# Layer norm's scaling and the turned maxima's copy on ScalarE, two pieces of VectorE's behind the next maxima, in a two-layer block

## Time and profile before

| | us |
|---|---|
| median of 3 runs (1610.04 to 1612.97) | 1611.84 |
| the profiled execution's own time | 1606.22 |
| its span, first to last instruction | 1604.5 |
| TensorE, VectorE, ScalarE, GpSimd busy | 1459.2, 1338.2, 1129.7, 578.4 |
| mean granted TensorE clock | 0.956 |

### The profile page before, as it was taken

One profiled execution on the slowest core, in us unless ns is written; L12 is line 12 of the kernel. 1 busy time (PEld: TensorE's weight loads), 2 busy tenths in 40 slices (PEclk: granted clock), 3 DMA queues, 4 the chain that ended last, 5 costly groups with the idle time before them and its releaser, 6 DMA issues.

```text
span 1604.5 us, 34217 instructions
## 1 busy us (share of the span) xinstructions
PE 1459.2 (91%) x10557; PEld 583.9 (36%) x10557; DVE 1338.2 (83%) x3450; ACT 1129.7 (70%) x2580; POOL 578.4 (36%) x531
## 2 busy tenths in 40 slices
PE   3978989999999899989999999989999988989986
PEld 1112344443333544432333444333433432323332
DVE  6999877789887698999888789889878779978991
ACT  2267678788787467777878767768878845765675
POOL 3002302103253456440242263660152464554443
PEclk8599999999999899999999999999999977989998
DMA  6403273333271452221451135123372100600000
GB/s 172 102 8 100 73 184 110 106 87 91 88 183 52 120 116 83 59 82 36 134 120 51 37 113 134 49 82 99 111 165 82 39 26 2 152 9 15 2 2 14
DMA packets 169833, 131.84 MB, mean 82 GB/s; under 512 B 31597, under 2 KB 143158, under 8 KB 169654
## 3 DMA queue, kind: packets, MB, share of 16 engines
q1 hardware_dynamic: 165562, 121.26, 28.5%
q0 software_dynamic: 4096, 8.40, 1.7%
HBM read 88.50 MB, written 40.50 MB: 80 GB/s over the span
## 4 chain that ended last, share of the span: by engine, by line
PE 58%; DVE 26%; issue 6%; ACT 5%; POOL 3%; DMA 1%; SPq 0%; another core or an unknown queue 0%; DVEq 0%; ACTq 0%; POOLq 0%
PE ring L542 38%; PE pO L542 17%; DVE mparts L1201 15%; PE ring L545 3%; ACT PR L854 3%; DVE junk L1205 2%; DVE xr L1381 1%; DVE stats L1251 1%; ACT hid L925 1%; DVE hs L1493 1%; DVE xr L1501 1%; DVE am L1414 1%; DMA b1r<-in_b 1%; ACT parts L548 0%; DVE hs L1489 0%
## 5 line engine op out<-in xcount | busy, mean ns | idle before, releaser
L854 ACT ACTIVATE PR<-ring 128x512 f32<-128x512 f32 (+3 forms) x1792 | 882.4, 557 | 344.8 <-PE ring L542 333.7
L1201 DVE TENSOR_REDUCE mparts<-ring 128x1 f32<-128x512 f32 x1280 | 808.5, 682 | 84.4 <-PE ring L542 77.1
L542 PE MATMUL ring<-QX,KX 50*128 50x512 bf16 (+3 forms) x1792 | 543.7, 366 | 77.2 <-DVE mparts L1201 35.5
L542 PE MATMUL ring<-KX,QX 48*128 48x512 bf16 (+3 forms) x1792 | 556.8, 374 | 14.2 <-DMA QX<-scratch 14.1
L542 PE MATMUL pO<-PR,VX 128*18 128x512 f32 (+3 forms) x3584 | 444.0, 568 | 6.5 <-ACT PR L854 5.2
L542 PEld LDWEIGHTS ring<-QX,KX 50*128 50x128 bf16 x1792 | 127.5, 94 | 609.0 <-ACT PR L854 220.3
L1205 DVE CUSTOM_DVE_ANT_0 junk<-ring,diag 128x384 bf16<-128x384 f32 (+3 forms) x512 | 228.8, 486 | 46.0 <-PE ring L542 41.2
L811 POOL TENSOR_SCALAR bq<-bq 128x352 f32<-128x352 f32 (+1 forms) x40 | 47.2, 1179 | 349.7 <-ACT bq L964 349.3
L784 POOL DMA_INDIRECT rows_in<-xn,at x64 | 63.7, 996 | 228.8 <-PE pO L542 144.8
L542 PEld LDWEIGHTS ring<-KX,QX 48*128 48x128 bf16 x1792 | 127.3, 94 | 33.6 <-DVE mparts L1201 17.9
L925 ACT ACTIVATE hid<-ring,b1r 128x128 f32<-128x128 f32 x368 | 105.0, 369 | 27.7 <-PE ring L542 26.2
(11 more groups left out here) (165 smaller groups left out, 1349.8 us busy)
## 6 DMA issues: line engine op xcount, KB each, us to landing
w1r<-in_w SPq DMA_DIRECT2D x92, 256.0 KB
w2r<-in_w SPq DMA_DIRECT2D x92, 256.0 KB
scratch<-parts SPq DMA_DIRECT2D x48, 256.0 KB, 3.3
scratch<-parts SPq DMA_DIRECT2D x96, 128.0 KB, 2.3
KX<-scratch SPq DMA_DIRECT2D x64, 192.0 KB, 4.4
QX<-scratch SPq DMA_DIRECT2D x128, 96.0 KB, 5.0
xg<-rows_in SPq DMA_DIRECT2D x92, 64.0 KB
rows_out<-yx SPq DMA_DIRECT2D x92, 64.0 KB
```

The source lines that it names most:

```text
L542: return nc.tensor.matmul(dst, lhsT, rhs, start=start, stop=stop, **kw)
L854: nc.scalar.activation(PR[:, n % 2, HALF * j + off:HALF * j + HALF], ring[plan.bank("E", k)][:, off:HALF], ACT.Exp, scale=SCALE).then_inc( ...
L1201: v.tensor_reduce(dst, src[:, 0:w], axis=X, op=ALU.max).then_inc(s_mr, 1)
```

## The change

1. **Norms.** VectorE's `var` step also computes `less = -mean`. GpSimd, after the power, computes `shift = less * rstd`; the power first waits until the phase before's norms are done. The norm becomes one ScalarE instruction per token tile, `xn = Identity(rstd * x + shift)`, in `late`, behind the slot's exponentials and pieces; ScalarE takes over the waits that VectorE had. In phases 3 to 6 a pair goes to the next slot where ScalarE's planned work is at most 8; in phases 1, 2 and 7 two pairs go in each of two slots; in phase 0 all four in one.
2. **mtr's copy** is done by ScalarE, in its xs; its planned cost is 5 and counts for ScalarE.
3. **Combine.** The high part is a second reduction straight from the parts; it doesn't wait for the first. VectorE waits until TensorE has turned the combine before.
4. **Deferral.** In each slot VectorE's xs from the first `gu` or layer-1 `pj` on are left over, and done in the next slot behind maxima 0 and 1.
5. VectorE's additions of `fp`, and of the first `down`, to the residual wait for the phase's norms, in both layers.

The pieces' own code (`piece(e)`) is what stood in the loop, but for `mtr` and point 5.

```diff
-ON_VECTOR = ("pj", "lg", "rt", "mtr", "fin", "gu", "down", "fp")
+ON_VECTOR = ("pj", "lg", "rt", "fin", "gu", "down", "fp")
...
-         "pj": 11, "mtr": 8, "fin": 15, "gu": 8, "down": 5, "fp": 11, "lg": 5, "rt": 5}
+         "pj": 11, "mtr": 5, "fin": 15, "gu": 8, "down": 5, "fp": 11, "lg": 5, "rt": 5}
...
-        i = self.chain("ln", i + 1, [("norm", p, t) for t in range(0, T, 2)], 1, room)[-1]
+        i += 1
+        for t in range(0, T, 2):
+            while room and self.busy(i, "A") and self.busy(i, "A") > 8:
+                i += 1
+            self.slot(i)["late"].append(("norm", p, t))
+            i += 1 if room or (p and t % TH) else 0
         for h in range(NH):
             i = self.put(i + 1, ("xT", p, h), 3)
...
                             pool.wait_ge(s_var, p + 1)
+                            if p:
+
+                                pool.wait_ge(s_xn, T * p)
                             nc.gpsimd.tensor_tensor(rstd[:, :], var[:, :], minus_half[:, :], ALU.pow).then_inc(s_rstd, 1)
+                            pool.wait_ge(s_rstd, 2 * p + 1)
+                            nc.gpsimd.tensor_tensor(shift[:, :], less[:, :], rstd[:, :], ALU.mult).then_inc(s_rstd, 1)
...
+                        if e[0] == "mtr":
+                            k = plan.mtrs[e[1:]]
+                            if k:
+                                act.wait_ge(s_row, 64 * k)
+                            copy(mT[:, :], src[0:2 * G * TH, 0:P]).then_inc(s_freed["A"], 1)
...
+                        if e[0] == "norm":
+                            _, p, t0 = e
+                            layer, b = PHASES[p]
+                            act.wait_ge(s_rstd, 2 * p + 2)
...
+                            for t in (t0, t0 + 1):
+                                nc.scalar.activation(xn[layer][:, t, :], xr[b % NX][:, t, :], ACT.Identity,
+                                                     bias=shift[:, t:t + 1], scale=rstd[:, t:t + 1]).then_inc(s_xn, 1)
...
                     if kind == "var":
                         own()
+                        count(v.tensor_scalar(less[:, :], mv[:, :, 0], -1.0, None, ALU.mult))
+                        own()
                         v.tensor_scalar(var[:, :], mv[:, :, 1], EPS, None, ALU.add).then_inc(s_var, 1)
-                    if kind == "norm":
...
-                            v.tensor_scalar(xn[layer][:, t, :], src[:, t, :], mv[:, t, 0:1], rstd[:, t:t + 1],
-                                            ALU.subtract, ALU.mult).then_inc(s_xn, 1)
...
+                left_over = []
                 for s in plan.slots:
                     maxima(s, (0, 1))
+                    for e in left_over:
+                        piece(e)
                     for e in s["small"][0] + s["small"][1]:
                         small_step(e)
                     maxima(s, (2, 3))
                     if s["combine"] is not None:
                         layer = PHASES[s["combine"][0]][0]
                         dve.wait_ge(s_mr, 4 * (plan.quads[s["quad"]] + 1))
-                        link(v.tensor_reduce(mneg[:, :], mparts[layer][:, s["combine"][2], :, :], axis=X, op=ALU.max,
-                                             negate=True))
-                        link(v.tensor_copy(msplit[:, 0:G * TH], mneg[:, :]))
+                        n = plan.combines[s["combine"]]
+                        if n:
+
+                            dve.wait_ge(s_x, filled(("mtr",) + list(plan.combines)[n - 1]))
+                        parts_ = mparts[layer][:, s["combine"][2], :, :]
+                        count(v.tensor_reduce(mneg[:, :], parts_, axis=X, op=ALU.max, negate=True))
+                        link(v.tensor_reduce(msplit[:, 0:G * TH], parts_, axis=X, op=ALU.max, negate=True))
                         v.tensor_tensor(msplit[:, G * TH:2 * G * TH], mneg[:, :], msplit[:, 0:G * TH],
                                         ALU.subtract).then_inc(s_ng, 1)
...
+                    mine = [e for e in s["xs"] if plan.by[e][0] == "D"]
+                    late = [e[0] == "gu" or (e[0] == "pj" and e[4] == "") for e in mine]
+                    n_now = late.index(True) if True in late else len(mine)
+                    for e in mine[:n_now]:
+                        piece(e)
+                    left_over = mine[n_now:]
                     for e in s["small"][3]:
                         small_step(e)
```

More of the change, by code:

```diff
@@ L408, in two_layer_block @@
         rstd = sb("rstd", [P, T])
+        less = sb("less", [P, T])
+        shift = sb("shift", [P, T])
         ra = sb("ra", [P, 2, HALF])
@@ L956, in _ @@
                             copy(parts[:, q, 1, HALF * h:HALF * h + HALF], left(n)).then_inc(s_mid, 1)
+                        if e[0] == "norm":
+                            _, p, t0 = e
+                            layer, b = PHASES[p]
+                            act.wait_ge(s_rstd, 2 * p + 2)
+                            if t0 == 0 and b:
+                                was = PHASE_OF[layer, b - 1]
+                                act.wait_ge(s_x, filled((("xT", "xqT")[layer], was, NH - 1)))
+                                if layer == 0:
+                                    act.wait_ge(s_sc[b - 1], 16 * 2 * T)
+                            for t in (t0, t0 + 1):
+                                nc.scalar.activation(xn[layer][:, t, :], xr[b % NX][:, t, :], ACT.Identity,
+                                                     bias=shift[:, t:t + 1], scale=rstd[:, t:t + 1]).then_inc(s_xn, 1)
                         if e[0] == "gates":
@@ L1241, in small_step @@
                     kind = e[0]
-                    if kind in ("stats", "means", "var", "norm"):
+                    if kind in ("stats", "means", "var"):
                         p = e[1]
@@ L1427, in small_step, with piece @@
                                                    wide(ri, width), ALU.mult, ALU.mult).then_inc(s_yq, 1)
+                def piece(e):
+                    src = bank(e)
+                    if e[0] != "gu" or e[3]:
+                        dve.wait_ge(s_x, filled(e))
+                    if e[0] == "pj":
+                        _, p, q, h, part = e
+                        n = plan.parts[p, q, h]
+                        half = slice(HALF * h, HALF * h + HALF)
+                        if n >= 4:
+                            dve.wait_ge(s_lo, n - 1)
+                        if part == "a":
+                            ins = v.tensor_tensor(sums(n), src[:, :], rc[:, half], ALU.mult)
+                        elif part == "b":
+                            ins = v.tensor_tensor(left(n), src[:, :], rs[:, half], ALU.mult)
+                        else:
+                            dve.wait_ge(s_hi, n + 1)
+                            ins = v.tensor_tensor(left(n), src[:, :], parts[:, q, 0, half], ALU.subtract)
+                    if e[0] == "lg":
+                        ins = v.tensor_tensor(logit[:, :, :], src[:, 0:T * E].rearrange("p (t e) -> p t e", e=E),
+                                              gb[:, :].rearrange("p (o e) -> p o e", o=1).to_broadcast([P, T, E]),
+                                              ALU.add)
+                    if e[0] == "rt":
+                        ins = v.tensor_copy(before[:, :], src[:, 0:E * 2 * T + E])
+                    if e[0] == "fin":
+                        _, p, g, qh = e
+                        o4 = src[:, :].rearrange("p (q j w) -> p q j w", j=G, w=OW)
+                        link(v.reciprocal(linv[:, :, :, :], o4[:, :, :, DK:2 * VC:VC]))
+                        if g == 0 and (p or qh):
+                            dve.wait_ge(s_x, filled(("of", p if qh else p - 1, 1 - qh)))
+                        for i in range(2):
+                            dst = otok[:, :, G * DK * (2 * g + i):G * DK * (2 * g + i) + G * DK]
+                            inv = linv[:, :, :, i].rearrange("p q (j o) -> p q j o", o=1).to_broadcast([P, TH, G, DK])
+                            ins = v.tensor_tensor(dst.rearrange("p q (j w) -> p q j w", w=DK),
+                                                  o4[:, :, :, VC * i:VC * i + DK], inv, ALU.mult)
+                    if e[0] == "gu":
+                        _, p, t, up = e
+                        if up:
+                            ins = v.scalar_tensor_tensor(hs[:, :], hs[:, :], 0.5, src[:, 0:F1], ALU.mult, ALU.mult)
+                        else:
+                            dve.wait_ge(s_th, T * PHASES[p][1] + t + 1)
+                            dve.wait_ge(s_yq, plan.pools["hq", p, t])
+                            ins = v.scalar_tensor_tensor(hs[:, :], th[:, :], 1.0, src[:, 0:F1], ALU.add, ALU.mult)
+                    if e[0] in ("down", "fp"):
+                        _, p, i = e
+                        b = PHASES[p][1]
+                        own()
+                        dst = xr[b % NX][:, i, :] if e[0] == "down" else flat(xr[b % NX], i)
+                        if e[0] == "fp" or i == 0:
+                            dve.wait_ge(s_xn, T * (p + 1))
```

(6 more changed lines are left out.)

69 lines of the change are left out of this document (removed).

## The result

The changed kernel took 1642.58 us, median of 4 runs (1640.65 to 1652.07), beside 1611.32 of the kernel before on the same chip: ratio 1.0218, 95% interval [1.0178, 1.0258]. It is 2.2% slower; I had forecast 1.2% faster. The profiled execution took 1640.65, span 1638.9, granted clock 0.953.

The account below looks back on a forecast made before the run. No single engine bounds it; TensorE leads the chain at 58%, fed through seven banks that VectorE or ScalarE empties. Terms summed to -20.1 us from 1611.84: forecast 1591.7 us, chance 0.48, range 1572 to 1615.

Parts of the forecast that it names:

- deferral of gu: VectorE's 25 waits for the tanh, 21.5 us, filled with the next maxima 0 and 1; at 0.4, -8.6 us.
- ScalarE's rate for the norms: Cost per us of ScalarE's time on 56 norms: taken as 0.2, +4.1 us, bounds 0.07 and 0.5.
- My slower case: ScalarE's queue becomes the late one, in front of the exponentials: +4.9 us, 1616.7; chance 0.18.
- deferral of pj, with `mid`: Layer 1's projections: 10.6 us of VectorE waits at 0.4, -4.2; ScalarE's `mid` waiting behind maxima, +1.5.
- norms: VectorE, `less`, ScalarE, start: Norms leaving VectorE -8.0 us, `less` +0.4, norms on ScalarE +4.1, longer kernel start +1.7.
- turned copy and combine: Copy leaving VectorE -5.3 us, arriving on ScalarE +1.3; combine's cast replaced by a second reduction -3.0.
- My first rival: Deferred pieces' banks hold TensorE up for as long as VectorE waited, both deferrals worth nothing: 1604.5 us; chance 0.18.
- my 7.6 us: What VectorE gives back without the norms: -8.0 us, less +0.4 for the added `less` instructions.
- The slower rival: Same as My slower case: norms, turned copies and a waiting `mid` hold up ScalarE's exponentials; 1616.7 us, chance 0.18.
- my bound of 11.0: Upper bound in us on ScalarE's `mid` waiting for a deferred piece: all 16 waits by 0.69; 1.5 was taken.
- The start: Phase 0's norms at the kernel's start have no cover; `flip` at 13.2 to 13.9 against 12.19: +1.7 us.
- The planner: Pieces are shuffled and some loads come two slots later, taken as covered; some 5 us either way.

Follow-up runs that it names:

- replanned: Kernel before with only the turned copy on ScalarE and the second reduction in the combine, the planner told of the new cost: ratio 1.0003.
- the form with the old plan: Kernel before with the turned copy on ScalarE and the second reduction, every slot planned as before: ratio 0.9975 and, again, 0.9963.
- another kernel: Kernel before with norms still on VectorE but in the change's slots: 1.0071; with phase 5's norms and turns back in slots 269 to 286: 1.0013.

## Why the prediction was wrong

It was wrong in sign, by two terms: the deferral of gu, which I priced as a gain, and ScalarE's rate for the norms. My slower case ended at 1616.7. It had the place right for the norms, and wrong for the deferral.

| term | forecast, us | measured, us |
|---|---|---|
| deferral of gu | -8.6 | +29.6 alone |
| deferral of pj, with `mid` | -2.7 | +1, open by 9 either way |
| both deferrals | -11.3 | +30.7 alone, +20 within the change |
| norms: VectorE, `less`, ScalarE, start | -1.8 | +18 |
| turned copy and combine | -7.0 | -4.0 and -5.9; replanned +0.5 |

(Measured: the ratio's excess times 1600; +20 is 1.3%.) The parts multiply to more than the whole: 1.0112 x 1.0003 x 1.0192 = 1.031 against 1.0218. The difference, 0.9%, is about as large as these intervals leave open, so whether the deferral costs less beside the others is not shown.

- **Deferral of gu, the step that failed.** I wrote that the gate's bank is freed two maxima later and that TensorE's seventh filling waits for it, and then priced the step at 0.4 of VectorE's wait, with bounds of 0 and -21.5. No bound was above zero. The held bank was a cost of its own, not a discount on a gain: +29.6 us by itself. It could have been bounded before: 59 slots of the plan hold a gate or an up piece, and two maxima take 1.27 us in the timeline above, so with no spare bank it is up to 75 us. In the trace the banks stand 0.85 us (gate) and 1.04 us (up) longer, 60 us for the 32 of each. The runs that take the deferral out, put it in alone, for gu alone, and behind one reduction, and the timeline, show the mechanism. My first rival, waits that change places at no net cost, had TensorE's waits right in kind and too small: some 13 us forecast for its waits for `hs` and `rb`, 33.0 measured of matmuls alone (0.5 before).
- **Why a wait did not buy its length.** VectorE's wait for the tanh was 21.5 us in 25 pieces, 0.86 us on average, and seven of the 32 gate pieces had none to speak of. The 32 up pieces never waited for ScalarE, and were put off all the same; TensorE waits for them as well (9.6 us of matmuls, 16.3 of weight loads). What took the place of a wait is 1.3 us of maxima, whether there had been a wait or not.
- **Norms, the second step that failed.** Duration: 0.482 us, not 0.369. The row I took has one operand per partition. The Trainium skill (ScalarE: Activation LUTs, "What ACT_TABLE_LOAD costs") adds about 93 ns for each; my estimate of 462 ns, that on top of my row, is 4% under the trace. As the norms overlap where they follow each other, ScalarE is busy for 27.0 us with all 64, 3.18 of them at the start: 23.8 us for 56, where I had 20.7. So the duration is the small part. Rate: the 56 cost, net of what VectorE gives back, some 16 us. That is 0.67 of ScalarE's time, and about 1 if VectorE gave back my 7.6 us. My 0.2 for ScalarE was far too kind, although I had named the cause: the next exponentials stand behind them, and TensorE behind those. ScalarE's 333.7 us of idle come in 440 pieces, 0.76 us on average; hardly any holds a block of 3.18 us.
- **The slower rival** put its price on one place, in front of the exponentials, and would decide at a ScalarE rate of 0.37. The norms by themselves passed that, so for them it was right. The turned copies did not: the form with the old plan gained. `mid` was late as it said (ScalarE's waits for `rb` rose from 0.8 to 9.9 us, near my bound of 11.0), but what that cost is lost in the 9 us that the pj deferral is open by. The Trainium skill (ScalarE: Activation LUTs, "Rules for kernel authors"), by which add and multiply belong on VectorE, points the way the norms' runs went, by 1.1%.
- **The start**: +1.7 forecast, 1.67 at `flip`, 2.2 by its ratio (which alone is within the noise). Right. The norms wait for GpSimd there alone, as I had assumed (8.5 us, once).
- **The turned copy and the combine**: right in kind, and in size within what two runs show: -4.0 and -5.9 for -7.0. In the combine, the reduction in the cast's place saved 3.8 us of VectorE's time and 2.2 us of idle time instead of the 9.6 that I took for both, and the subtraction behind it took 1.7 us more (0.230 against 0.203 us).
- **The planner**: I allowed 5 us either way. The replanning seems to have taken back the turned copy's 4 to 6 us, and one phase's shift cost 0.58% in another kernel. I had not looked where phase 5 would go: its turns came ten slots earlier, onto a phase change.
- **Busy times**: VectorE 1306 for a forecast of some 1290, ScalarE 1160 for 1171. They moved the way I forecast, by two thirds and three quarters of the size, and said nothing of the time.

## What to carry to other kernels

Moving a read of a PSUM bank behind other work changes how long the bank is held: in a ring without a spare bank, bound it by that time for each occurrence, on the engine that fills the bank, and set it against the wait it saves; here it was the larger (29.6 us lost, of 60 us that banks stood longer, for 21.5 us of waits). Put off only the reads that had waited. Idle time of an engine is of use only in pieces as long as what is to go in. When a planner places work by costs, an edit that changes a cost is two edits: measure it with the plan held still.

## What the runs showed of the hardware

- ScalarE with scale and bias per partition on 128x128 in fp32: 477/482/550 ns, against a mean of 369 ns for the expert's activation with a bias alone. VectorE's form of the same norm had a median of 341 ns. For this shape ScalarE is the slower engine by 0.14 us. VectorE's had a longest of 1100 ns and a mean of 401; on ScalarE none took more than 550.
- GpSimd on a 128x8 tile: 204 ns for a multiplication, 1674 ns for the power.
- ScalarE's copy of 32x128 out of PSUM to bf16 took 254 ns, VectorE's 269.
